# First layer norm of a 16-head attention: statistics by token before the turn, in place of centring and summing products after it

## The reference

```python
def _layernorm(x, axis=-1, eps=1e-05):
    m = jnp.mean(x, axis=axis, keepdims=True)
    v = jnp.var(x, axis=axis, keepdims=True)
    return (x - m) / jnp.sqrt(v + eps)
...
    x = x + _L0_attn_a_ref(_layernorm(x, axis=-1), L0_attn_a_w_qkv, ...)
```

## Time and profile before

| | |
|---|---|
| median of 3 runs | 1131.77 us (1130.97 to 1134.86) |
| profiled execution, span from first to last instruction | 1128.3 us |
| median less span: start and end around the span | 3.5 us |
| PE busy | 1008.2 us, 89% |
| DVE busy | 804.1 us, 71% |
| ACT busy | 721.7 us, 64% |
| POOL busy | 386.2 us, 34% |
| mean granted clock of PE | 0.920 |

### The profile page before, as it was taken

One profiled execution on the slowest core, in us unless ns is written; L12 is line 12 of the kernel. 1 busy time (PEld: TensorE's weight loads), 2 busy tenths in 40 slices (PEclk: granted clock), 3 DMA queues, 4 the chain that ended last, 5 costly groups with the idle time before them and its releaser, 6 DMA issues.

```text
span 1128.3 us, 21762 instructions
## 1 busy us (share of the span) xinstructions
PE 1008.2 (89%) x8208; PEld 603.0 (53%) x8208; DVE 804.1 (71%) x1234; ACT 721.7 (64%) x1501; POOL 386.2 (34%) x267
## 2 busy tenths in 40 slices
PE   4989999989857899999999899898989999999996
PEld 2423333332215667667666566565656666666652
DVE  1766565656328879889887777686869889888751
ACT  2357566656644776776776657575657687687662
POOL 2100103001016555445453344343335535545410
PEclk9968788787788999999999899898989999999998
DMA  2200000000003111011010000000001011011100
GB/s 63 61 13 2 1 1 1 2 1 1 1 19 91 26 25 29 16 26 30 16 26 21 15 21 16 18 17 11 20 15 24 22 25 25 21 24 35 30 15 15
DMA packets 25218, 23.65 MB, mean 21 GB/s; under 512 B 10610, under 2 KB 17052, under 8 KB 25116
## 3 DMA queue, kind: packets, MB, share of 16 engines
q1 hardware_dynamic: 25116, 22.27, 8.5%
HBM read 6.16 MB, written 1.05 MB: 6 GB/s over the span
## 4 chain that ended last, share of the span: by engine, by line
PE 48%; DVE 14%; issue 4%; ACT 2%; POOL 2%; DVEq 0%; POOLq 0%
PE psum L1145 8%; PE psum L1117 5%; PE psum L1078 5%; PE psum L1019 4%; PE psum L1153 4%; PE psum L1057 4%; PE psum L1029 3%; PE psum L1067 3%; PE psum L1021 3%; PE psum L1020 3%; DVE f_NM L1404 3%; DVE f_A L1372 2%; DVE f_BS L1376 2%; DVE f_SS L1383 2%; DVE f_PT L1396 2%
## 5 line engine op out<-in xcount | busy, mean ns | idle before, releaser
L948 POOL TENSOR_TENSOR f_A<-f_A,f_BS 128x1024 f32<-128x1024 f32 x64 | 151.0, 2359 | 231.4 <-DVE f_BS L1376 231.1
L659 DVE TENSOR_REDUCE a_M<-psum 128x2 f32<-128x1024 f32 x128 | 152.9, 1219 | 85.8 <-PE psum L498 85.1
L609 ACT ACTIVATE a_PT<-psum 128x1024 f32<-128x1024 f32 x128 | 129.8, 1023 | 79.2 <-PE psum L508 76.7
L953 POOL TENSOR_TENSOR f_A<-f_A,f_RN 128x1024 f32<-128x1024 f32 x64 | 121.8, 1904 | 109.3 <-ACT f_RN L1262 108.5
L1251 ACT ACTIVATE f_PW<-psum,f_NM 128x128 f32<-128x128 f32 x512 | 138.9, 382 | 13.9 <-DVE f_NM L1404 10.9
L1404 DVE TENSOR_REDUCE f_NM<-psum 128x4 f32<-128x512 f32 x128 | 81.9, 679 | 53.2 <-PE psum L1057 53.2
L1372 DVE TENSOR_TENSOR f_A<-psum,cos 128x512 f32<-128x512 f32 x128 | 87.7, 685 | 42.8 <-ACT f_SQ L1217 42.8
L1078 PE MATMUL psum<-f_VS,f_PT 128*64 128x65 f32 x1024 | 82.2, 229 | 39.3 <-DVE f_PT L1396 18.2
L1217 ACT ACTIVATE f_SQ<-psum 128x512 f32<-128x512 f32 x128 | 75.4, 608 | 61.1 <-PE psum L1021 57.0
L1078 PEld LDWEIGHTS psum<-f_VS,f_PT 128*64 128x64 f32 x1024 | 68.6, 140 | 72.3 <-issue 42.9
L508 PE MATMUL psum<-a_QS,a_KS 25*128 25x512 f32 x256 | 73.4, 568 | 27.5 <-DVE a_M L659 22.6
(11 more groups left out here) (165 smaller groups left out, 2019.7 us busy)
## 6 DMA issues: line engine op xcount, KB each, us to landing
f_VS<-f_V SPq DMA_DIRECT2D x112, 130.0 KB, 2.3
raw<-L_ffn_wqkv_dram SPq DMA_DIRECT2D x2, 768.0 KB, 5.8
a_XT<-L_attn_a_x_dram SPq DMA_DIRECT2D x4, 256.0 KB, 3.2
a_QS<-a_MROW SPq DMA_DIRECT2D x64, 2.0 KB, 1.7
out_dram<-f_OUT SPq DMA_DIRECT2D x4, 256.0 KB, 2.3
f_w<-L_ffn_w_dram SPq DMA_DIRECT2D x2, 341.0 KB
tables<-const_dram SPq DMA_DIRECT2D x1, 512.0 KB, 4.1
f_wo<-L_ffn_wo_dram SPq DMA_DIRECT2D x8, 64.0 KB
```

What stands on the lines that cost most here:

```text
L609: nc.scalar.activation(PT[:, h:h + 2, t, :], psum[:, pair("by_key", i), :], ACT.Exp, scale=float(DA) ** -0.5).then_inc(s("exped"), 1)
L659: nc.vector.tensor_reduce(M[:, quads % 2, t, 2 * j:2 * j + 2], psum[:, pair("scores", i), :], AX_X, ALU.max).then_inc(s("maxed"), 1)
L948: nc.gpsimd.tensor_tensor(A[:, k % 2, :, :], A[:, k % 2, :, :], BS[:, k % 2, :, :], ALU.add)\
L953: nc.gpsimd.tensor_tensor(x, x, RN[:, k % 2, :, None].to_broadcast([P, 2 * HW, DW]), ALU.mult)\
```

## The change

The mean and the variance of each token are taken from the tile as loaded, where a token is one partition: DVE runs bn_stats and bn_aggr on each of the four parts (`MV`), ACT makes one over the root of four columns of variances (`RS`). For the first sequence DVE centres and scales with one tensor_scalar for each part; for the others POOL subtracts the mean and multiplies, each in one instruction of 512 columns, into `XN`. PE turns `XN` (`turn_n`, four transposes) and ACT copies it to `XC`. The entries `center_x` and `var_x` go; `stats` (slot -31) and `turn_n` (slot -27) come. The copy into `X` by `turn_x` stays, since the attention's result is added to it. `SELECT` and the cast of the constants move behind the first sequence's `turn_n` and `stats`. SP's next load into an `XT` buffer also waits until the tile has been centred.

```diff
-AROUND = sorted([(-32, "turn_x", 0), (-29, "center_x", 0), (-27, "var_x", 0), (-21, "queries_keys", 0),
+AROUND = sorted([(-32, "turn_x", 0), (-31, "stats", 0), (-27, "turn_n", 0), (-21, "queries_keys", 0),
...
+             "turn_x": (("x_copied", lambda i: i + 1),), "turn_n": (("xc", lambda i: i + 1),),
...
                     if work == "turn_x" and i + 2 < SEQS:
                         sp.wait_ge(s("x_turned"), i + 1)
+                        sp.wait_ge(s("centered" if i else "normed"), 1)
                         load(XT[:, i % 2, :, :], x_of(i + 2), f"x_loaded{i % 2}")
... POOL
-                    if work == "var_x":
-                        if n:
-                            pool.wait_ge(s("projected_v"), n)
-                        normalize(number["x", n], XC[:, :], "xc")
+                    if work == "stats" and n:
+                        pool.wait_ge(s("stats"), n + 1)
+                        pool.wait_ge(s("n_turned"), n)
+                        nc.gpsimd.tensor_tensor(XN[:, :, :], XT[:, n % 2, :, :],
+                                                MV[:, :, 0:1].to_broadcast([P, 4, P]), ALU.subtract)\
+                          .then_inc(s("centered"), 1)
+                        pool.wait_ge(s("centered"), n)
+                        pool.wait_ge(s("rstd"), n + 1)
+                        nc.gpsimd.tensor_tensor(XN[:, :, :], XN[:, :, :],
+                                                RS[:, n % 2, :, None].to_broadcast([P, 4, P]), ALU.mult)\
+                          .then_inc(s("normed"), 1)
... PE
+                    elif work == "turn_n":
+                        pe.wait_ge(s("normed"), i + 1)
+                        dst = take("turn_n", i)
+                        for t in range(4):
+                            last = nc.tensor.transpose(dst[:, P * t:P * t + P], XN[:, t, :], ident)
+                        last.then_inc(s("n_turned"), 1)
... ACT
-                act.wait_ge(s("const_a"), 16)
-                nc.scalar.activation(SELECT[:, :, :], cst("select").rearrange("p (i x) -> p i x", i=4), ACT.Copy)\
-                  .then_inc(s("select"), 1)
...
+                    elif work == "stats":
+                        if i == 0:
+                            act.wait_ge(s("eps"), 2)
+                        act.wait_ge(s("stats"), i + 1)
+                        if i >= 2:
+                            act.wait_ge(s("normed"), i - 1)
+                        nc.scalar.activation(RS[:, i % 2, :], MV[:, :, 1], ACT.Ln, bias=g.eps[:, 0:1])\
+                          .then_inc(s("var_log"), 1)
+                        act.wait_ge(s("var_log"), i + 1)
+                        nc.scalar.activation(RS[:, i % 2, :], RS[:, i % 2, :], ACT.Exp, scale=-0.5)\
+                          .then_inc(s("rstd"), 1)
+                    elif work == "turn_n":
+                        act.wait_ge(s("n_turned"), i + 1)
+                        if i:
+                            act.wait_ge(s("projected_v"), i)
+                        nc.scalar.activation(XC[:, :], psum[:, bank("turn_n", i), :], ACT.Copy).then_inc(s("xc"), 1)
+                        if i == 0:
+                            act.wait_ge(s("const_a"), 16)
+                            nc.scalar.activation(SELECT[:, :, :], cst("select").rearrange("p (i x) -> p i x", i=4),
+                                                 ACT.Copy).then_inc(s("select"), 1)
... DVE
-                dve.wait_ge(s("const_a"), 16)
-                dve.wait_ge(s("tables"), 16)
-                nc.vector.tensor_copy(g.constb[:, :], constb_f).then_inc(s("tables_cast"), 1)
-                dve.wait_ge(s("tables_cast"), 1)
                 for work, i in plan:
-                    if work[:6] == "center":
+                    if work == "stats":
+                        dve.wait_ge(s(f"x_loaded{i % 2}"), 16 * (i // 2 + 1))
+                        if i:
+                            dve.wait_ge(s("rstd"), i)
+                        if i >= 2:
+                            dve.wait_ge(s("centered"), i - 1)
+                        for t in range(4):
+                            last = nc.vector.bn_stats(STATS[:, t, :], XT[:, i % 2, t, :])
+                        last.then_inc(s("parts"), 1)
+                        dve.wait_ge(s("parts"), i + 1)
+                        for t in range(4):
+                            last = nc.vector.bn_aggr(MV[:, t, :], STATS[:, t, :])
+                        last.then_inc(s("stats"), 1)
+                        if i == 0:
+                            dve.wait_ge(s("rstd"), 1)
+                            for t in range(4):
+                                last = nc.vector.tensor_scalar(XN[:, t, :], XT[:, 0, t, :], MV[:, t, 0:1],
+                                                               RS[:, 0, t:t + 1], ALU.subtract, ALU.mult)
+                            last.then_inc(s("normed"), 1)
+                            dve.wait_ge(s("const_a"), 16)
+                            dve.wait_ge(s("tables"), 16)
+                            nc.vector.tensor_copy(g.constb[:, :], constb_f).then_inc(s("tables_cast"), 1)
+                            dve.wait_ge(s("tables_cast"), 1)
```

More of the change, by code:

```diff
@@ L266, in attention_a @@
             singles += [(work[:-2], number[work[-1], i])]
-        elif work not in ("scores", "by_key", "sums_2"):
+        elif work not in ("scores", "by_key", "sums_2", "stats"):
             singles += [(work, i)]
@@ L278, in attention_a @@
     FREED = {"scores": (("maxed", lambda i: i + 1),), "by_key": (("exped", lambda i: i + 1),),
-             "turn_x": (("x_copied", lambda i: i + 1),),
+             "turn_x": (("x_copied", lambda i: i + 1),), "turn_n": (("xc", lambda i: i + 1),),
              "center": (("ln_kept", lambda i: i + 1),),
@@ L302, in attention_a @@
         LR = sb("LR", [P, T])
+        XN = sb("XN", [P, 4, P])
+        STATS = sb("STATS", [P, 4, 6])
+        MV = sb("MV", [P, 4, 2])
+        RS = sb("RS", [P, 2, 4])
         XC = sb("XC", [P, T])
@@ L453, in _ @@
                         last.then_inc(s("x_turned"), 1)
+                    elif work == "turn_n":
[4 more added lines that the diff above has]
+                        last.then_inc(s("n_turned"), 1)
                     elif work[:6] == "center":
-                        pe.wait_ge(s("x_copied" if work[-1] == "x" else "x_added"), i + 1)
+                        pe.wait_ge(s("x_added"), i + 1)
                         x = number[work[-1], i]
@@ L563, in _ @@
                         x = number[work[-1], i]
-                        if x == 0:
-                            act.wait_ge(s("eps"), 2)
                         act.wait_ge(s("var"), x + 1)
                         if x:
-                            before, m = norms[x - 1]
-                            act.wait_ge(s("xc" if before == "x" else "y_new"), m + 1)
+                            act.wait_ge(s("y_new"), norms[x - 1][1] + 1)
                         nc.scalar.activation(LR[:, :], psum[:, bank("var", x), :], ACT.Ln, scale=1.0 / P,
@@ L634, in _ @@
             def _(dve):
-                dve.wait_ge(s("const_a"), 16)
-                dve.wait_ge(s("tables"), 16)
-                nc.vector.tensor_copy(g.constb[:, :], constb_f).then_inc(s("tables_cast"), 1)
-                dve.wait_ge(s("tables_cast"), 1)
                 for work, i in plan:
-                    if work[:6] == "center":
+                    if work == "stats":
[21 more added lines that the diff above has]
+                            dve.wait_ge(s("tables_cast"), 1)
+                    elif work[:6] == "center":
                         x = number[work[-1], i]
@@ L643, in _ @@
                         if x >= 2:
-                            before, m = norms[x - 2]
-                            dve.wait_ge(s("xc" if before == "x" else "y_new"), m + 1)
+                            dve.wait_ge(s("y_new"), norms[x - 2][1] + 1)
                         nc.vector.tensor_copy(CEN[:, x % 2, :], psum[:, bank("center", x), :]).then_inc(s("ln_kept"), 1)
```

## The result

The median of the changed kernel is 1120.51 us (four executions, 1119.58 to 1121.67), beside 1131.37 for the kernel before (four, 1130.28 to 1134.86): a ratio of 0.9906, interval 0.9890 to 0.9922. The forecast was 1121.8. The profiled execution of after took 1121.67 us with a span of 1119.6; that of before had a span of 1128.3.

A forecast was written before the change was run, and what follows sets the result against it. The prediction took a serial start of 17 us, then PE (89% busy) at a changing clock, as the bound. Gains of 7.5 + 2.5 + 0 = 10.0 us gave 1128.3 - 10.0 + 3.5 = 1121.8 us, range 1114 to 1129.

The forecast's parts named there:

- The start: Chain before sequence 0's projection: projection at 9.4 us instead of 16.9, 7.5 us earlier, ends 5.8 to 7.6.
- Slots 0 to 11: Scores of sequence 0: PE saves 3.0 us, less about half of DVE's added 0.9; 2.5 us gained, ends 0 and 3.0.
- The norms inside sequences 1 and 2: Norms for sequences 2 and 3: less PE work brings a slower PE; 0 each, ends 3.0 gained and 2.9 lost.
- Slot 31 to 95: Sign over sequences 1 and 2: the forecast is wrong if this distance moves by over 3 us either way.
- Rival (a): Sequences 1 and 2: work taken from PE counts in full, 1.6 to 3.0 us each, say 1117; chance 0.22.
- Rival (b): Sequences' start: full clock shrinks from 20.5 to 10.2 us, each sequence up to 2.9 us longer; 1127.6; chance 0.20.
- Rival (c): Start and later norms: DVE's small instructions cost far more than 0.2 us; at 1.25 each, 1155; chance 0.05.
- Rival (d): Start: another input, weights or biases, holds the projection, so part of that gain could go; with the rest, chance 0.03.
- The sum: Whole kernel: 7.5 + 2.5 + 0 = 10.0 us gained, forecast 1121.8 us with chance 0.50.

The follow-up runs named there:

- e4: Changed kernel, with ACT taking Ln and Exp of the first sequence's variances ahead of the copy of X; 1118.24 us, ratio 0.9877 to the kernel before.
- e3: Changed kernel, with the old centring and summing products put back idle on PE for sequences 1 to 3; 1122.93 us, ratio 0.9917 to the kernel before.
- e7: Changed kernel, with one idle product at the old centring's slot for sequences 1 to 3; 1121.25 us, ratio 0.9905 to the kernel before.
- the repeated run: The changed kernel once more, unaltered, timed beside other experiments; 1120.13 us, ratio 0.9895 to the kernel before.
- e8: Changed kernel, with eight idle transposes of X at the old centring's slot for sequences 1 to 3; 1116.34 us, ratio 0.9867 to the kernel before.
- e10: Changed kernel, with eight idle transposes for each of sequences 1 to 3 and Ln and Exp ahead of the first copy of X; 1116.31 us, ratio 0.9864.
- e9: e4 with two idle products of 384 columns in every quad from slot 16 on; 1128.45 us, ratio 0.9963 to the kernel before.

## Why the prediction was right, point by point

**The start**, 7.5 us: 7.0 in the first profile, 7.2 in the second, inside the ends of 5.8 to 7.6. The statistics came a microsecond earlier than counted, because x is there at 3.41 and they need no identity, and this gave nothing: ACT copies X first, and Ln starts at 6.36, where the sum had about 6.2; the identity landed at 4.71 in this execution instead of 4.41. The eight small instructions took 1.25 us instead of 1.6, hidden; the four that centre and scale took 1.12 instead of 0.8, on the path; Ln 0.29 instead of 0.216. e4 shows that the copy of X, which the sum had in its path, need not be there: without it the projection starts 1.0 to 1.3 us earlier.

**Slots 0 to 11**, 2.5 us with an upper end of 3.0: 3.5. This is the term that was mis-sized. What was taken away counted in full, 4.1 us (e3, e7). What was added, the four transposes (1.11 by duration) and DVE's 0.9, cost 0.6 together: e3, which has PE's old and new work, takes 19.45 us against 18.87 before. I had set transposes against products one for one and added half of DVE's share, 1.6 in all. That the path moves towards DVE is borne out: DVE is full in this stretch now (14.99 of 15.34 us). How 0.5 us of the transposes' 1.11 come to cost nothing was not shown.

**The norms inside sequences 1 and 2**, 0 us each with ends of 3.0 gained and 2.9 lost: 71.6 to 74.0 and 71.7, against 71.8 and 71.7. The reason given, that less work brings a slower PE, is what e3 shows: the same kernel with the products has twice the full clock and the same length. Slot 31 to 95 moved by 2.3 us in the first profile and by -0.2 in the second, within the 3 that were named. The 0 itself was the middle of a gain of 0.9 and a loss of 1.5, not a sum; that what the first eight slots of a sequence lose comes back in the next eight (below) was not foreseen, and that the two come out even is luck.

**Rival (a)**, the PE work in full, falls (its best end is 1115.2 by the terms given, not 1114): putting it back into sequences 1 and 2 costs nothing there, and the 2.8 us that e3 is above the repeated run are less than its loss in slots 0 to 11. **Rival (b)** had the mechanism right (10.2 us instead of 20.5) and the price wrong in three sequences of four; the kernel with the shorter stretch gets most of it back in the quad behind. Slots 31, 39 and 47 of the repeated run show it:

```profile
74.94 1.23 DVE L709 TENSOR_REDUCE a_M<-psum 128x2 f32<-128x1024 f32 x1 [3.83 <-PE psum L516]
...
92.19 1.23 DVE L709 TENSOR_REDUCE a_M<-psum 128x2 f32<-128x1024 f32 x1 [3.25 <-PE psum L516]
...
110.08 1.22 DVE L709 TENSOR_REDUCE a_M<-psum 128x2 f32<-128x1024 f32 x1 [3.35 <-PE psum L516]
```

The first eight slots take 17.3 us, 1.2 more than before (16.1), and the next eight 17.9; e3, with its long stretch, takes 15.9 and then 19.3. So the price that (b) read from the first part of a sequence is there, and the part behind it pays it back. That the weighted sums of the last sequence fall into the slow stretch can't be read from the earlier trace rows, but the trace of before has them from 242.3 us on, where the clock is at 0.50. **Rival (c)** is out by the groups above: 157 to 344 ns, none near 1.25 us. **Rival (d)** is out by the timeline: nothing holds the projection but its own copy.

The rule of the Trainium skill ("TensorE: Matmul & The Clock Gate", Part 4), that the full clock does not engage for transposes as for matmuls, does not hold for this kernel: by e8 and e10 transposes added among the score products lengthen the stretch at granted clock 1.00 from 10.2 to 13.6 us and more, as far as a product does (20.5 in e7). A stretch of transposes with no products beside them was not run.

**The sum**: 10.0 us predicted, 8.7 between the two profiled spans: 10.3 up to slot 31 (7.0 and 3.5, less 0.2), 2.3 lost in sequence 1, 0.2 lost over the last sequence and its end, 0.9 gained in the stage behind. That slot 31 came at 75.3 with 75.6 forecast is in part luck: the start gained 0.5 less than counted and slots 0 to 11 gained 1.0 more. The medians differ by 10.9 and 12.6. Here the spread of before is larger than what is left over, so how much of the 0.9 to 2.6 us beyond the forecast gain belongs to the change stays open.

## What to carry to other kernels

Statistics by token that need only the tile as loaded take a chain out of a start where nothing runs beside it, and there they count by their durations, provided that no engine stands in front of a constant that it needs later. Where PE stayed at the lower level (slots 0 to 11), PE work taken away counted in full, until DVE was as full as PE. Where its clock comes and goes (sequences 1 and 2), it was worth nothing by itself: read the granted clock ahead of and behind the place before counting it. A little idle work where a full-clock stretch begins can be worth more than the work saved, as eight transposes were here; one product there gained nothing in all, and products in every quad made the kernel 8 to 10 us slower.

## What the runs showed that was not expected

- Idle transposes, eight for each of sequences 1 to 3, make the kernel 3.8 us faster (1116.34 against 1120.13); with the root first it is no faster (1116.31, 0.9864 of the kernel before).
- Stretches whose work is unchanged move with the clock: the last sequence, which has no norm to prepare, takes 65.8 us in four profiles and 68.6 in four others, and its end 38.7 or 36.2, one for the other (65.8 and 38.7 in after, 68.6 and 36.2 in e3).
- The kernel before takes between 1121.8 and 1135.1 us in these executions, the change 1118.83 to 1121.67: in its ten executions the change has the smaller spread, and e9 a wide one again (1118.0 to 1131.0).
- Two POOL passes with a broadcast operand take 1.04 us each, not the 1.27 of the pass with two full operands.
